# Attention's side job moved to the end of the iteration, and the joined preparation stage cut into two phases

## The reference, cut to what matters

```
q = rmsnorm((norm(x) @ Wq).reshape(B, 512, 16, 128)); k = rmsnorm(ctx @ Wk ...); v = ctx @ Wv ...
x = x + softmax(q k^T * scale) v @ Wo                    # attention, 16 heads in 8 pairs
x_up, x_gate = fwht(x * SU_ug) @ W_up.T, ... @ W_gate.T  # needs W_up, W_gate turned
h = silu(x_gate) * x_up
x = x + fwht(h * SU_dp) @ W_down.T * Wscale_dp           # the rotation is folded into W_down beforehand
u = silu(conv4(in_proj @ ctx) + conv_b)                  # per batch: u, delta, du, B, C for the scan
dt, Bm, Cm = split(x_proj @ u); delta = softplus(dt_proj @ dt + dt_bias); du = delta * u
```

## Time and profile before

| | before |
|---|---|
| device time, median of 3 runs | 2864.66 us (2862.95 to 2866.11) |
| the profiled execution's own time | 2869.26 us |
| its span, first to last instruction | 2867.5 us |
| busy over the span: PE, PEld | 2312.4 us (81%), 1762.5 us |
| busy over the span: DVE, ACT, POOL | 1895.9 us (66%), 1246.9 us, 1354.0 us |
| attention, prep, mixer, the rest behind | 69 to 1349, 1350 to 1564 (the next stage's first instruction at 1569), to 2345, to 2867 us |

### The profile page before, as it was taken

How to read it: one execution, slowest core, us unless ns; L and a number is a source line. 1 busy time by engine, 2 the same in 40 slices (tenths; PEclk the granted TensorE clock), 3 DMA queues, 4 the chain that set the end, 5 groups by cost and what they waited for, 6 DMA issues and landing times. The chain is left out here.

```text
span 2867.5 us, 37898 instructions
## 1 busy us (share of the span) xinstructions
PE 2312.4 (81%) x10784; PEld 1762.5 (61%) x10785; DVE 1895.9 (66%) x3615; ACT 1246.9 (43%) x2130; POOL 1354.0 (47%) x1722
## 2 busy tenths in 40 slices
PE   3799989989898989996655699898997948558981
PEld 2677777777777777875422466565665525437771
DVE  6577767767676767765433799999999974422323
ACT  2344444444444444443444465565654612114430
POOL 0233333333332333331640678888878922378424
PEclk7799999999999999998667799999999968779996
DMA  6512222211323221222323756466464411475416
GB/s 265 199 63 89 81 104 82 97 63 67 104 81 104 82 78 68 81 81 60 117 89 133 226 172 205 148 194 202 162 191 152 149 53 55 142 214 179 139 51 249
DMA packets 136076, 363.84 MB, mean 127 GB/s; under 512 B 21184, under 2 KB 58816, under 8 KB 117440
## 3 DMA queue, kind: packets, MB, share of 16 engines
q1 hardware_dynamic: 122784, 328.36, 34.0%
q0 software_dynamic: 6320, 20.71, 2.3%
q10 hardware_dynamic: 6768, 12.32, 1.1%
HBM read 290.06 MB, written 71.30 MB: 126 GB/s over the span
## 5 line engine op out<-in xcount | busy, mean ns | idle before, releaser
L1778 POOL TENSOR_TENSOR mix_drive<-mix_du,mix_rows 128x512 f32<-128x512 f32 x256 | 326.9, 1284 | 151.9 <-DMA mix_rows<-bc_d 119.4
L662 POOL TENSOR_SCALAR att_probs<-att_probs,att_recip 128x512 f32<-128x512 f32 x256 | 184.5, 725 | 378.8 <-DVE att_recip L743 368.2
L585 ACT ACTIVATE att_probs<-att_s,att_bias,att_rq 128x512 f32<-128x512 f32 x256 | 200.2, 782 | 300.9 <-DVE att_bias L739 298.6
L1831 DVE TENSOR_TENSOR_SCAN mix_state<-mix_state,mix_drive 128x512 f32<-128x512 f32 x256 | 312.7, 1221 | 15.1 <-POOL mix_drive L1778 10.0
L1662 ACT ACTIVATE mix_state<-mix_delta,mix_a 128x512 f32<-128x512 f32 x256 | 176.8, 692 | 278.2 <-DVE mix_drive L1842 238.3
L1763 POOL TENSOR_TENSOR mix_y<-mix_y,mix_drive 128x512 f32<-128x512 f32 x180 | 230.7, 1282 | 78.3 <-DVE mix_drive L1842 78.3
L1571 PE MATMUL mix_down<-mix_wd,mix_hT 128*128 128x512 f32 x512 | 232.2, 596 | 8.6 <-DVE residual_x L1862 8.6
L789 DVE TENSOR_TENSOR att_pT<-att_pt,att_pT 128x512 fp32r<-128x512 f32 x256 | 172.6, 685 | 79.4 <-ACT att_pT L591 79.0
L591 ACT CAST att_pT<-att_pt 128x512 fp32r<-128x512 f32 x256 | 147.4, 589 | 172.5 <-PE att_pt L442 168.5
L738 DVE TENSOR_REDUCE att_nmax<-att_s 128x1 f32<-128x512 f32 x256 | 175.0, 684 | 64.6 <-PE att_s L101 64.4
L442 PE MATMUL att_pt<-att_ident,att_probs 128*128 128x128 f32 x1024 | 150.6, 277 | 50.1 <-DVE att_ffnT L794 48.0
(11 more groups left out here) (355 smaller groups left out, 6779.4 us busy)
## 6 DMA issues: line engine op xcount, KB each, us to landing
att_xn<-normT SPq DMA_DIRECT2D x32, 2048.0 KB
mix_gu<-guT SPq DMA_DIRECT2D x64, 1024.0 KB
mix_rows<-bc_d SPq DMA_DIRECT2D x128, 256.0 KB, 5.3
guT<-att_ffnT SPq DMA_DIRECT2D x32, 512.0 KB, 3.5
mix_wd<-wdT SPq DMA_DIRECT2D x16, 1024.0 KB
slots<-exp_y ACTq DMA_DIRECT2D x47, 256.0 KB
normT<-nrm_outT SPq DMA_DIRECT2D x4, 2048.0 KB, 10.1
exp_raw<-in_L_ffn_Wg SPq DMA_DIRECT2D x16, 512.0 KB
```

Of the source, the lines that this page charges most:

```text
L585: act.activation(probs[:, n, :], ps_s[n % 2][:, :], ACT.Exp, bias=bias[:, n:n + 1], scale=rq[:, n:n + 1], accum_out=sums[:, n:n + 1]).then ...
L662: pool.tensor_scalar(probs[:, n, :], probs[:, n, :], recip[:, n:n + 1], 1.0, ALU.mult, ALU.mult).then_inc(s_pn, 1)
L1778: pool.tensor_tensor(drive[q % RING][:, :], du[i % DUS][:, :], rows[g % ROWS][:, 0, :], ALU.mult).then_inc(s_drive, 1)
L1831: dve.tensor_tensor_scan(h[:, :], h[:, :], drive[q % RING][:, :], 0.0, ALU.mult, ALU.add).then_inc(s_scan, 1)
```

## The change

In attention the side job moves behind the first two scores of j and ahead of `project` on PE, to the end of the iteration on ACT (behind `exp(j, 1)`), and behind `row_max(j, 1)` and ahead of the four `add_y` on DVE. The bank numbering follows, and SP's waits name the later counts.

In the preparation stage all 16 down rounds come first, with the small weight turns put in after rounds 5, 7, 9 and 11, then the channel strand in a schedule of slots. W_down has four buffers instead of two (no load waits), the butterflies work in them, `rotate_down` alternates two banks, the first scaled tile no longer waits for all constants, and `scale_down` goes from ACT to DVE. `channels`/`convolve` get three buffers, `spread` moves on DVE from the stage's start to behind the down rounds, and the last batch's Ln, `step_sizes` and stores go tile by tile.

```diff
@@ attention: SP, PE, ACT, DVE
-                        sp.wait_ge(s_pt, TURNS * i + TB + 1)
+                        sp.wait_ge(s_pt, TURNS * i + TURNS)
                         load_ffn(hp + (b + 1) // B, (b + 1) % B)
-                    sp.wait_ge(s_ptlo, TURNS * i + TB + 1 + 2)
+                    sp.wait_ge(s_ptlo, TURNS * i + TURNS + 2)
                     store_ffn(hp, b)
...
-                    turn_ffn(hp, i, b)
                     turn_p(i, b, 1, 0)
                     turn_p(i, b, 1, 1)
...
                         score(j, 0)
                         score(j, 1)
+                    turn_ffn(hp, i, b)
                     pe.wait_ge(s_olo, 2 * i + 4)
...
-                    ffn_hi(hp, i, b)
                     for k in range(TB):
                         pt_hi(i, b, 1, k)
...
                         exp(j, 0)
                         exp(j, 1)
+                    ffn_hi(hp, i, b)
...
-                    ffn_lo(i, b)
                     pt_lo(i, b, 1, 0)
...
                         row_max(own, j, 1)
+                    ffn_lo(i, b)
                     for t in range(TB):
                         add_y(i, b, t)
@@ prep: PE
+                pe.wait_ge(s_ident, 16)
+                turn_down(0)
+                turn_down(1)
                 pe.wait_ge(s_had, 1)
+                for n in range(KD * AG):
+                    rotate_down(n)
+                    if n + 2 < KD * AG:
+                        turn_down(n + 2)
...
+                    if n >= KD * AG - 3:
+                        channels(n - (KD * AG - 3))
                 pe.wait_ge(s_te, KC + 2)
+                for s in range(B * ET + 4):
+                    b, t = divmod(s - ET, ET)
+                    if s + 3 < B * ET:
+                        channels(s + 3)
+                    if b >= 0:
+                        if t == 0:
+                            low_rank(b)
+                        if t == 1:
+                            step_size(b, 0)
+                            step_size(b, 1)
+                        if t == 2:
+                            step_size(b, 2)
+                            step_size(b, 3)
+                    if s < TB:
+                        turn(s)
+                    if 8 <= s < 8 + KD:
+                        rotate(s - 8)
@@ prep: ACT
+                for n in range(KD * AG):
+                    down_out(n)
+                    if n + 2 < KD * AG:
+                        down_hi(n + 2)
...
+                for s in range(B * ET + 4):
+                    b, t = divmod(s - ET, ET)
+                    if s < TB:
+                        norm(s)
+                    if s < B * ET:
+                        u(s // ET, s % ET)
+                    if 1 <= s <= TB:
+                        norm_out(s - 1)
+                    if b >= 0:
+                        if t == 1:
+                            low_rank(b)
+                        if t == 2:
+                            parts(b, 0)
+                            parts(b, 1)
+                        if t == 3:
+                            parts(b, 2)
+                            parts(b, 3)
+                            softplus(b)
+                    if 9 <= s < 9 + KD:
+                        rotated(s - 9)
@@ prep: DVE
+                def scale_down(k):
+                    dve.wait_ge(s_wraw[k], 16)
+                    dve.tensor_scalar(wraw[k][:, :], wraw[k][:, :], dsc[:, k:k + 1], None, ALU.mult).then_inc(s_ws, 1)
...
+                for n in range(KD * AG):
+                    down_lo(n)
+                    if n == 0:
+                        scale_down(1)
+                    if n == 4:
+                        scale_down(2)
...
+                    if n == 8:
+                        scale_down(3)
...
                 spread()
...
+                for s in range(B * ET):
+                    convolve(s // ET, s % ET)
+                    if s >= 8 and s % ET == 0:
+                        step_sizes((s - 8) // ET)
+                    if 9 <= s < 9 + KD:
+                        rotated_lo(s - 9)
+                step_sizes(B - 2)
                 step_sizes(B - 1)
```

More of the change, by code:

```diff
@@ L943, in stage_prep @@
         cx = [m.sb(f"cx{i}", [P, 2, KC, S], F32R) for i in range(2)]
-        conv = [m.sb(f"conv{i}", [P, S]) for i in range(2)]
+        conv = [m.sb(f"conv{i}", [P, S]) for i in range(3)]
         us = [m.sb(f"u{i}", [P, ET, S]) for i in range(2)]
@@ L959, in stage_prep @@
         normT = wraw[0][:, :].rearrange("p (k n) -> p k n", k=KD)
-        ps_x = [m.ps(f"x{i}", [P, S]) for i in range(2)]
+        ps_x = [m.ps(f"x{i}", [P, S]) for i in range(3)]
         ps_d = m.ps("dbl_ps", [P, S])
@@ L963, in stage_prep @@
         turned = [m.ps(f"turned{i}", [P, DIM]) for i in range(2)]
-        rot = m.ps("rot", [P, DIM])
-        s_const, s_in = m.sem("const_in"), m.sem("weights_in")
+        s_dsin, s_ident, s_hin, s_su, s_in = (m.sem(f"{n}_in") for n in ("dscale", "ident", "had", "su", "weights"))
         s_had, s_hs, s_dsc = m.sem("had_rounded"), m.sem("had_signed"), m.sem("dscale_done")
-        s_wraw = [m.sem(f"wraw_in{i}") for i in range(2)]
+        s_wraw = [m.sem(f"wraw_in{k}") for k in range(KD)]
         s_ws, s_dt, s_dhi, s_dlo = m.sem("w_scaled"), m.sem("down_turned"), m.sem("down_hi"), m.sem("down_lo")
@@ L1047, in _ @@
                 store_bc(3)
-                store_delta(3)
-                for q in s_st:
-                    sp.wait_ge(q, 16 * B)
+                for t in range(ET):
+                    store_last_delta(t)
+                sp.wait_ge(s_st[0], 16 * B)
+                for q in s_st[1:]:
+                    sp.wait_ge(q, 16 * (B - 1 + ET))
                 for i in range(2):
@@ L1100, in step_size @@
                         pe.wait_ge(s_relu, n - 1)
+                    else:
+                        pe.wait_ge(s_dout, KD * AG)
                     pe.matmul(ps_z[n % 2][:, :], dtT[:, t * P:(t + 1) * P], dbl[0:RANK, :], start=True,
@@ L1167, in _ @@
             @block.scalar
             def _(act):
-                def scale_down(k):
-                    if k == 0:
-                        act.wait_ge(s_dsc, 1)
-                    act.wait_ge(s_wraw[k % 2], 16 * (k // 2 + 1))
-                    act.activation(wraw[k % 2][:, :], wraw[k % 2][:, :], ACT.Copy, scale=dsc[:, k:k + 1]).then_inc(s_ws, 1)
                 def down_hi(n):
@@ L1183, in down_out @@
                     act.wait_ge(s_dr, n + 1)
-                    if k >= 2 and g == 0:
-                        act.wait_ge(s_wst, 16 * (k - 1))
-                    act.copy(fly[k % 2][:, g * DIM:(g + 1) * DIM], rot[:, :]).then_inc(s_dout, 1)
+                    act.copy(wraw[k][:, g * DIM:(g + 1) * DIM], ps_z[n % 2][:, :]).then_inc(s_dout, 1)
                 def u(b, t):
@@ L1219, in softplus @@
                         act.wait_ge(s_delta, b)
-                    act.activation(soft[:, :, :], mag[:, :, :], ACT.Ln, bias=1.0).then_inc(s_soft, 1)
+                    if b < B - 1:
+                        act.activation(soft[:, :, :], mag[:, :, :], ACT.Ln, bias=1.0).then_inc(s_soft, 1)
+                    else:
+                        for t in range(ET):
+                            act.activation(soft[:, t, :], mag[:, t, :], ACT.Ln, bias=1.0).then_inc(s_soft, 1)
                 def norm(t):
@@ L1251, in _ @@
-                act.wait_ge(s_t, KC + 2)
-                act.copy(dtT[:, :], ps_d[0:RANK, :]).then_inc(s_te, 1)
-                scale_down(1)
-                for r in range(B + 1):
-                    if r:
-                        low_rank(r - 1)
-                    for t in range(ET):
-                        n = 2 * (ET * r + t)
-                        if r < 2:
-                            if n + 2 < KD * AG:
-                                down_hi(n + 2)
-                            down_out(n + 1)
-                        if n == 4 or n == 8:
-                            scale_down(n // 4 + 1)
-                        if r < B:
-                            u(r, t)
-                        if r < 2 and n + 3 < KD * AG:
-                            down_hi(n + 3)
-                            down_out(n + 2)
-                        if r:
-                            parts(r - 1, t)
-                        if r == 2:
-                            norm(t)
-                            norm_out(t)
-                        if r == 3:
-                            rotated(t)
-                    if r:
-                        softplus(r - 1)
+                for n in range(KD * AG):
+                    down_out(n)
+                    if n + 2 < KD * AG:
+                        down_hi(n + 2)
+                    if n == 5:
+                        act.wait_ge(s_t, 1)
+                        act.copy(inT[:, 0, 0, :], ps_d[:, :]).then_inc(s_te, 1)
+                    if n == 7:
+                        act.wait_ge(s_t, 2)
+                        act.copy(inT[:, 0, 1, :], ps_d[:, :]).then_inc(s_te, 1)
+                    if n == 9:
```

(7 more changed lines are left out.)

209 lines of the change are left out of this document (90 added, 119 removed).

## The result

The changed kernel's median is 2914.1 us (2912.5 to 2922.4 in 4 runs) beside 2863.8 us of the kernel before: ratio 1.018, 95% interval 1.016 to 1.021, some 50 us slower (50 between the medians, 52 by the ratio). I had forecast 2837, faster. The profiled execution has a span of 2911.8 us, 44.3 more than before. All of it lies in the two stages: from the last residual add of attention to the next stage's first instruction 202.2 us where it was 219.9, so the preparation gained 17.7 us; the last add itself ends at 1411.2 instead of 1349.2, so attention lost 62.0.

A forecast was written before the change was run, and what follows sets the result against it. PE was taken to bound attention, hand-overs the preparation. Attention +15.5 us and preparation -43.5 us summed to -28 us, giving 2837 us on the median of 2864.66; 2810 to 2860 was to hold 8 in 10.

The forecast's parts named there:

- Attention, regular steps: Attention, queries to queries within a pair: PE waits 1.1 us for `add_y`, 1.9 for `xn`; steps grow +0.9 to +1.1 us.
- `xn` is in time: Rival: attention's `xn` load arrives before the queries need it, attention gains 20 us, kernel 2801; chance 0.09.
- Attention, back edge: Attention, step over the loop's back edge: `xn` arrives within the 30.1 us available, so the step is 0.8 us shorter.
- both nothing: Attention: the weights at b = 0 and the tile load go out well ahead of use and cost nothing.
- Cover gone they would cost as `xn` does: Attention: weights and tile load, if no longer issued ahead of their need, would cost like the late `xn` load.
- Preparation, first turn: Start of preparation: PE's first turn at 1357.4 instead of 1364.98, waiting only for `dscale` and the first tile.
- Phase one: Preparation's down rounds: sixteen rounds 27.2 us, small turns 4, constants 1, three scalings 3.9; ends at 1393.5.
- Preparation, `spread` and the matrices: Preparation, between down rounds and first convolution: this DVE work now lies bare, 6.1 + 1.7 us.
- some 5: Preparation's down rounds: the last two scalings could each wait one butterfly, 2.5 us more, making them some 5 us longer.
- Phase two: Preparation from the first convolution on: 119 us, ending at 1520.3 against 1563.86.
- the rival of PE at the low clock: Preparation from the first convolution: PE stays at the low clock and becomes the bound; saving 22, kernel 2858; chance 0.15.
- The rival that ends slower: Attention: the late `xn` load takes from 10.5 us instead of 9.0, gain lost, kernel 2875; chance 0.06.

## Why the prediction was wrong, point by point

**Attention, regular steps: right.** `turn_p` and its chain are earlier, PE waits for `add_y` (forecast 1.1 us, measured 1.04) and for `xn` (1.9; 1.8), and a step grows by 1.05 where I had 0.9 to 1.1. That it fits so well is in part luck: 0.2 us of the 1.05 is PE's own work at the lower clock (busy 35.85 us a step for 35.63), a term that I did not have. Two readings were a little off: the third regular step is 38.4 us, not 38.2, and the back edge 42.3, not 42.5. The rival "`xn` is in time" was rightly set low; of its gain of 20 us 14 were measured over the whole kernel once SP's order was changed.

**Attention, back edge: the step that failed.** "Over the back edge T to queries takes 30.1 us and `xn` needs only 16.9 + 1.0 + 9 to 10.4 us, so there the step is 0.8 us shorter", and of the weights "both nothing". Measured: +6.8 us a step, +40.9 in all, where I had -5.6 (for seven steps; there are six, the seventh pair leaves the loop without a jump). I looked only at when data are needed. The earlier trace rows runs over 30 us in which the engines fetch their loop body, and I did not ask what the moved loads would share the DMA engines with. Nor did I have a term for PE's clock in attention, which fell behind the longer idle times: of the 6.8 us, 3.7 are PE's waits and 3.0 its work at a clock of 0.90. I had "Cover gone they would cost as `xn` does"; that was the wrong price as well, since nobody waits for these transfers. The Trainium skill, Runtime: NRT & Kernel Launch, Instruction fetch mechanics, says that a taken branch to a page that is not held forces a DMA fetch before execution goes on; the instruction packets of both traces agree, and a look there would have led to this question. What that fetch costs beside other traffic the page doesn't say; here DVE's idle time per fetch grew from 2.2 us to 5.4.

**Preparation, first turn: right** (8.2 us behind the last add, forecast 8.2). **Phase one** took 27.6 us, not 36: 8.5 us in my favour. I had added the small turns, a wait for constants and the scalings in line (8.9 us); that they fit between the rounds' hand-overs is argued, though moving three scalings to ACT changed the phase by only 0.2 us.

**Preparation, `spread` and the matrices: the second step that failed.** "Then DVE has `spread` and the signed matrices, 6.1 + 1.7 us" were prices from a stretch in which POOL did nothing. Beside the butterflies they cost 40.3, 32.5 us more. The earlier trace rows had the warning, 4.13 us against 2.29 with POOL beside it, and I put it on the scalings alone. There it was right: one scaling was held, 3.48 us for 1.28, two in the kernel with the preparation edit alone, and phase one took 3.1 and 4.7 us more than with the butterflies held back (24.5), where I had named some 5. The Trainium skill, SBUF — State Buffer, Who interferes with whom, also says that a VectorE instruction with two inputs in SBUF contends with a GpSimd instruction that reads SBUF, and, of the two-port modes, that the one who comes first holds the shared pair for its whole instruction. The 128x4 `tensor_tensor` at 2181 ns beside butterflies and 163 without them agree with it. The price of an operation that is held is then not its own length but what is left of the other's: in proportion, the smallest lose most.

**Phase two: right in sum**, 120.5 us from the first convolution to the last product, forecast 119. PE's clock is 0.75 over this stretch, so the rival of PE at the low clock did not come about as a bound on the sum, though DVE waits up to 10 us for a rotation in it.

The sum: the preparation was to save 43.5 us and saved 17.7 (-8.5 + 32.5 + 1.5 and some tenths); attention was to cost 15.5 and cost 62.0 (+46.5 at the back edge, +1.5 in the 24 regular steps, -1.6 at the ends). The rival that ends slower named the right place, SP's late loads, but the wrong mechanism: the load took 9.1 us in the median (7.7 to 12.2) where I had taken 9.0, and each regular step lost no more than forecast.

## What to carry to other kernels

Keep bulk transfers out of the few microseconds around a loop's back edge, even ones that nobody waits for: here 4 MB of them cost 7.5 us a jump, about half in instruction packets that start late and half in PE's lower clock behind the longer idle time. When a looped stage slows, look first at the idle time marked "issue", and then at the busy time and the granted clock of the same steps. An instruction that waits on a queue delays all that is issued behind it, so put the load that has a deadline ahead of the store that has none. Chains of small DVE operations on SBUF, such as the 128x4 ones here, belong where POOL is not working through long ones; a duration read in a quiet stretch is no price for a crowded one.

## What the runs showed of the hardware that I had not expected

- About 4 MB of stores that nothing waits for lengthen each of six back edges by 7.5 us (42.3 to 49.8). With `xn` early, the 1.5 MB of weights on the edge add 1.2 us (43.85 to 45.06).
- An instruction packet takes no longer beside 4 MB of traffic; it starts later, DVE's 3.1 to 4.5 us into its idle time instead of 0.3 to 0.6, and the engine goes on 1.2 to 1.7 us behind its end in either case.
- The profile counts a DVE operation that stands still beside a POOL operation as busy: 39.4 of 40 us, for operations that take 7.5 us together.
- After a wait of 1.96 us for `xn`, PE's granted clock was 0.50 from 739.2 to 742.0, the 1.2 GHz level, and the block's twelve instructions took 4.6 us instead of 3.0, and behind a wait of 1.83 us it was 0.62 from 864.6 to 868.0; at 700.3 and 826.2, after waits of 1.62 and 1.34 us, it stayed at 1.00. Six of the 24 waits (1.83 to 2.59 us) were followed by such a stretch, but waits of 2.77, 2.35 and 2.14 us were not. What decides between them stays open; it is inside the 1.05 us per regular step.
- In the kernel with `xn` early and the weights away, one 0.5 MB store that ends 0.5 us into PE's idle time is enough to make that idle time 3.0 us for 1.5, and 6.8 us or more at the 1.2 GHz level follow. That the store is the cause is read from the traces (its end and the packet's start lie within 0.3 us at all six edges); no run moved that store alone.
